# Routing of the expert stage: Silu times 1/x for the sigmoid, a power on GpSimd for 1/sqrt, PSUM operands and other places for VectorE's steps

## What is computed

```python
shared = silu(xf @ Ws_up) @ Ws_down
aff = xf @ centroids.T                       # xf: 4096 x 128, aff: 4096 x 64
_, idx = top_k(aff + expert_biases, 8)
w = sigmoid(take_along_axis(aff, idx, axis=1))
w = w / (sum(w, axis=-1, keepdims=True) + 1e-08)
cw = zeros((T, E)).at[arange(T)[:, None], idx].add(w)
h = silu(einsum('td,edf->etf', xf, W_up))    # 64 experts, F = 64
y = einsum('etf,efd->etd', h, W_down)
out = x + shared + einsum('etd,te->td', y, cw)
```

## Time and profile before

| | |
|---|---|
| median of 3 runs | 1102.46 us (1101.21 to 1103.21) |
| span of the profiled execution | 1102.4 us |
| its place among the runs | its own time is given by the span alone: 0.06 us below the median |
| TensorE busy | 948.5 us, 86% |
| VectorE busy | 845.6 us, 77% |
| ScalarE busy | 719.1 us, 65% |
| GpSimd busy | 446.7 us, 41% |
| expert stage | from 658.9 us to the end |

### The profile page before, as it was taken

How to read it: one execution, slowest core, us unless ns; L and a number is a source line. 1 busy time by engine, 2 the same in 40 slices (tenths; PEclk the granted TensorE clock), 3 DMA queues, 4 the chain that set the end, 5 groups by cost and what they waited for, 6 DMA issues and landing times.

```text
span 1102.4 us, 20447 instructions
## 1 busy us (share of the span) xinstructions
PE 948.5 (86%) x6019; PEld 747.6 (68%) x6052; DVE 845.6 (77%) x1938; ACT 719.1 (65%) x1416; POOL 446.7 (41%) x510
## 2 busy tenths in 40 slices
PE   4652099999658999999999979999999999999998
PEld 3541099999536677677767657676767676767676
DVE  6888177777567888888888657888787878787865
ACT  4650055555346877877777657777777778787776
POOL 1378650000156665565553403333333333333333
PEclk8655599999858999999999989999999999999999
DMA  8011122222210110100100008382838383838382
GB/s 250 26 49 61 50 57 67 63 65 66 66 32 21 30 30 23 33 25 24 35 21 20 1 7 194 71 207 62 189 80 196 73 189 74 192 77 192 79 193 72
DMA packets 63921, 89.99 MB, mean 82 GB/s; under 512 B 16559, under 2 KB 54610, under 8 KB 59730
## 3 DMA queue, kind: packets, MB, share of 16 engines
q1 hardware_dynamic: 59136, 80.33, 30.4%
q0 software_dynamic: 4096, 8.40, 2.7%
q10 hardware_dynamic: 594, 0.09, 0.0%
HBM read 70.90 MB, written 17.89 MB: 81 GB/s over the span
## 4 chain that ended last, share of the span: by engine, by line
PE 63%; DVE 12%; issue 7%; ACT 7%; POOL 7%; DMA 2%; SPq 1%; DVEq 0%; POOLq 0%; ACTq 0%
POOL xs L661 6%; PE ps L2146 4%; PE ps L2128 4%; PE ps L2130 4%; PE ps L2129 4%; PE ps L2148 4%; PE ps L2147 4%; PE ps L1932 3%; PE ps L1875 3%; PE ps L1956 3%; PE ps L1950 2%; PE ps L1995 2%; PE ps L1978 2%; PE ps L1854 2%; PE ps L1853 2%
## 5 line engine op out<-in xcount | busy, mean ns | idle before, releaser
L809 POOL TENSOR_TENSOR hl<-h,hh 128x512 fp32r<-128x512 f32 x128 | 165.6, 1294 | 292.1 <-ACT hh L1081 292.1
L1081 ACT ACTIVATE hh<-h 128x512 fp32r<-128x512 f32 (+1 forms) x264 | 165.1, 625 | 44.2 <-DVE h L1711 42.7
L1711 DVE TENSOR_TENSOR h<-ps,cwB 128x512 f32<-128x512 f32 x192 | 130.5, 680 | 45.3 <-ACT ps L1070 35.5
L1611 DVE TENSOR_REDUCE nm<-ps 128x4 f32<-128x512 f32 (+1 forms) x128 | 116.4, 951 | 35.7 <-PE ps L1978 33.8
L715 POOL DMA_INDIRECT yg<-ys,gps x64 | 63.0, 985 | 166.4 <-issue 155.9
L1070 ACT ACTIVATE ps<-ps 128x512 f32<-128x512 f32 x192 | 111.7, 582 | 26.2 <-PE ps L2130 25.6
L2146 PE MATMUL ps<-hh,wh 128*128 128x512 f32 x256 | 106.1, 414 | 11.4 <-DVE hl L1718 10.4
L2128 PE MATMUL ps<-xh,wh 128*128 128x512 f32 x256 | 105.0, 410 | 0.0
L2129 PE MATMUL ps<-xl,wh 128*128 128x512 f32 x256 | 101.6, 397 | 0.0
L2130 PE MATMUL ps<-xh,wl 128*128 128x512 f32 x256 | 101.4, 396 | 0.0
L2148 PE MATMUL ps<-hh,wl 128*128 128x512 f32 x256 | 101.3, 396 | 0.0
(11 more groups left out here) (326 smaller groups left out, 2692.3 us busy)
## 6 DMA issues: line engine op xcount, KB each, us to landing
cwB<-cwd SPq DMA_DIRECT2D x32, 1536.0 KB, 14.4
cwd<-cwS SPq DMA_DIRECT2D x64, 96.0 KB
xb<-xs SPq DMA_DIRECT2D x72, 64.0 KB, 1.8
ys<-yb SPq DMA_DIRECT2D x72, 64.0 KB, 1.6
x_res<-in_L_attn_x_dram SPq DMA_DIRECT2D x4, 512.0 KB, 6.8
wst<-in_L_ffn_W_up_dram SPq DMA_DIRECT2D x32, 64.0 KB, 2.2
wst<-in_L_ffn_W_down_dram SPq DMA_DIRECT2D x32, 64.0 KB, 1.9
out_dram<-y SPq DMA_DIRECT2D x8, 256.0 KB, 13.2
```

Source lines behind the costliest of these rows:

```text
L809: pool.tensor_tensor(hl4[:, slot(u), :], h4[:, slot(u), :], hh4[:, slot(u), :].bitcast(F32), op=ALU.subtract).then_inc(u_hlp, 1)
L1081: act.activation(hh4[r, slot(u), :], h4[r, slot(u), :], ACT.Copy).then_inc(u_hh, 1)
L1611: ins = dve.tensor_reduce(nm[:, u, 4 * g:4 * g + 4], o, axis=AX.X, op=ALU.max, negate=True)
L1711: dve.tensor_tensor(h4[:, slot(u), :], first, second, op=ALU.mult).then_inc(u_h, 1)
```

## The change

Tile 0's routing stays as it was. For the routings of tiles 1 to 7 (`first` is false):

- ScalarE takes Silu(x) of the logits instead of exp(-x), behind unit 17; VectorE divides by x (a reciprocal, L1564 before, and a multiplication more) to get the sigmoid. Logits so near to zero that adding 1e-20 gives 1e-20 are first moved off zero in two instructions (`near_zero`, `off_zero`). No table is loaded between the units.
- 1/sqrt(variance + 1e-5) is an addition and a power of -0.5 on GpSimd, behind its unit 5; ScalarE's ln and exp for it go.
- VectorE reads the tokens' low part, the logits and the biased logits directly from the PSUM bank; the copy of the logits goes. Since the low part now reads the bank that the logits overwrite, `x4_logits` on TensorE waits for it too (`d_hl`, named x4_parts).
- The last scaling writes the 48 columns that are spread straight to `cs` (`scaled`), and the rounding and the copy treat only the other 16 columns.
- The places move: normalization from behind unit 10 to 6, the transposes and their copy from 12 to 11, high and low part from 13 and 14 to 12 and 13, the reciprocal from 21 to 20, the last step from 28 to 27; logits stay at 14 and the transposes of the weights at 30.

```diff
@@ -22,6 +22,7 @@
 BIG = 1.0e30
+TINY = 1.0e-20
@@ -345,7 +347,7 @@
         SCATTERED = 16 * RT * K1
-        DVE_S, DVE_D = 4, 19
+        DVE_S, DVE_D, DVE_D1 = 4, 19, 20
@@ -437,6 +439,8 @@
             return bank[3] if isinstance(n, int) and n == 0 else bank[6]
+        X4_TURN, X4_LOGITS, X4_SILU, X4_SPREAD = 11, 14, 17, 30
@@ -802,12 +807,22 @@
+            def x4_rstd(n, p):
+                pool.wait_ge(d_mv, n + 1)
+                apart(pool, pool_passed)
+                pool.tensor_scalar(lnv[:, p, :], mv[:, p, :, 1], LN_EPS, None, ALU.add).then_inc(act_d, 1)
+                pool.wait_ge(act_d, n + 1)
+                pool.tensor_tensor(rstd[:, p, :], lnv[:, p, :], neg_half[:, :].broadcast_to([P, SUB]), op=ALU.pow).then_inc(d_rs, 1)
             def pool_tile(t, p, before, N, S):
                                        op=ALU.subtract).then_inc(u_hlp, 1)
+                    if u == 5 and S:
+                        x4_rstd(t + 2, p)
@@ -945,6 +960,10 @@
                 act.activation(g4[:, 0, :, :], af[:, :, :], ACT.Exp, scale=-1.0).then_inc(d_ex, 1)
+            def x4_silu(n):
+                act.wait_ge(d_afc, n + 1)
+                act.activation(g4[:, 0, :, :], af[:, :, :], ACT.Silu).then_inc(d_ex, 1)
@@ -1097,14 +1116,11 @@
                         out_copy4(before[0], before[1])
-                    if u == 12 and N:
+                    if u == X4_TURN and N:
                         x4_T(t + 1, 1 - p)
-                    if u == 16 and N:
-                        act.preload_act_table_set(TABLE)
-                        x4_exp(t + 1, 1 - p)
-                        if S:
-                            x4_rstd(t + 2, p)
-                    if u == 30 and N:
+                    if u == X4_SILU and N:
+                        x4_silu(t + 1)
+                    if u == X4_SPREAD and N:
                         x4_weights(t + 1, 1 - p)
@@ -1488,7 +1504,8 @@
-                own = Tickets(dve, dve_d, n * DVE_D)
+                first = isinstance(n, int) and n == 0
+                own = Tickets(dve, dve_d, 0 if first else DVE_D + (n - 1) * DVE_D1)
@@ -1504,8 +1521,52 @@
                     own.need(1)
-                    dve.tensor_tensor(xl4[:, p, :], flat(xnT4[:, :, :]), xh4[:, p, :].bitcast(F32),
+                    dve.tensor_tensor(xl4[:, p, :], flat(xnT4[:, :, :]) if first else x4_bank(n)[:, :], xh4[:, p, :].bitcast(F32),
                                       op=ALU.subtract).then_inc(d_hl, 1)
+                def logits():
+                    return x4_bank(n)[:, 0:SUB * E2].rearrange("p (k e) -> p k e", e=E2)
+                def near_zero():
+                    dve.wait_ge(d_af, n + 1)
+                    own.done(dve.tensor_scalar(g4[:, 2, :, :], logits(), TINY, TINY, ALU.add, ALU.is_equal))
+                def off_zero():
+                    own.need(own.n)
+                    dve.scalar_tensor_tensor(af[:, :, :], g4[:, 2, :, :], 2 * TINY, logits(), ALU.mult, ALU.add).then_inc(d_afc, 1)
+                def biased_logits():
+                    own.done(dve.tensor_tensor(bi[:, :, :], logits(), ebi[:, :].unsqueeze(1).broadcast_to([P, SUB, E2]), op=ALU.add))
+                def inverse_logits():
+                    dve.wait_ge(d_afc, n + 1)
+                    own.done(dve.reciprocal(g4[:, 3, :, :], af[:, :, :]))
+                def times_silu():
+                    dve.wait_ge(d_ex, n + 1)
+                    own.need(own.n)
+                    own.done(dve.tensor_tensor(g4[:, 4, :, :], g4[:, 2, :, :], g4[:, 0, :, :], op=ALU.mult))
+                def spread_columns():
+                    return cs[:, :, 0:EB].rearrange("p s (k h j) -> p s k h j", k=NPC, h=2)
+                def scaled():
+                    own.need(own.n)
+                    inverse = s4[:, 2, :].unsqueeze(2)
+                    own.done(dve.tensor_tensor(g4[:, 5, :, 0:EP], g4[:, 4, :, 0:EP], inverse.broadcast_to([P, SUB, EP]), op=ALU.mult))
+                    pairs = g4[:, 4, :, EP:E2].rearrange("p s (k j h) -> p s k h j", k=NPC, h=2)
+                    for half in range(2):
+                        dve.tensor_tensor(spread_columns()[:, :, :, half, :], pairs[:, :, :, half, :],
+                                          inverse.unsqueeze(3).broadcast_to([P, SUB, NPC, G]), op=ALU.mult)
+                def low_weights():
+                    own.need(own.n)
+                    dve.tensor_copy(cs[:, :, HB:HB + EP], cwh[:, :, 0:EP].bitcast(F32))
+                    dve.tensor_tensor(cs[:, :, HB + EP:HB + 2 * EP], g4[:, 5, :, 0:EP], cwh[:, :, 0:EP].bitcast(F32),
+                                      op=ALU.subtract).then_inc(d_cs, 1)
+                    assert own.n == DVE_D1, own.n
@@ -1560,12 +1621,18 @@
+                total = [then(lambda: dve.tensor_reduce(s4[:, 0, :], g4[:, 4, :, :], axis=AX.X, op=ALU.add)),
+                         then(lambda: dve.tensor_scalar(s4[:, 1, :], s4[:, 0, :], 1e-8, None, ALU.add)),
+                         then(lambda: dve.reciprocal(s4[:, 2, :], s4[:, 1, :]))]
+                if not first:
+                    return [norm, high, low, near_zero, off_zero, biased_logits, largest, replaced, chosen, inverse_logits,
+                            then(lambda: dve.tensor_tensor(g4[:, 2, :, :], g4[:, 3, :, :], g4[:, 1, :, :], op=ALU.mult)),
+                            times_silu, *total, scaled,
+                            then(lambda: dve.tensor_scalar(cwh[:, :, 0:EP], g4[:, 5, :, 0:EP], 0.0, None, ALU.add)), low_weights]
                 return [norm, high, low, affinity, biased, largest, replaced, chosen, sigmoid,
                         then(lambda: dve.tensor_tensor(g4[:, 4, :, :], g4[:, 3, :, :], g4[:, 1, :, :], op=ALU.mult)),
-                        then(lambda: dve.tensor_reduce(s4[:, 0, :], g4[:, 4, :, :], axis=AX.X, op=ALU.add)),
-                        then(lambda: dve.tensor_scalar(s4[:, 1, :], s4[:, 0, :], 1e-8, None, ALU.add)),
-                        then(lambda: dve.reciprocal(s4[:, 2, :], s4[:, 1, :])),
+                        *total,
                         then(lambda: dve.tensor_tensor(g4[:, 5, :, :], g4[:, 4, :, :],
@@ -1694,7 +1761,7 @@
-            STEP_AT = (10, 13, 14, 15, 16, 17, 18, 19, 20, 21, 22, 23, 24, 25, 26, 27, 28)
+            STEP_AT = (6, 12, 13, 15, 15, 16, 17, 18, 19, 20, 21, 22, 23, 24, 24, 25, 26, 27)
@@ -1910,6 +1978,8 @@
                 pe.wait_ge(d_Tc, n + 1)
+                if not (isinstance(n, int) and n == 0):
+                    pe.wait_ge(d_hl, n + 1)
                 for k in range(SUB):
@@ -2169,11 +2239,11 @@
                         out_T(before[0])
-                    if u == 12 and N:
+                    if u == X4_TURN and N:
                         x4_turned(t + 1, t if before is not None else None)
-                    if u == 14 and N:
+                    if u == X4_LOGITS and N:
                         x4_logits(t + 1)
-                    if u == 30 and N:
+                    if u == X4_SPREAD and N:
                         x4_weights(t + 1)
```

More of the change, by code:

```diff
@@ L90, in bass_two_layers @@
         eps_c = sb("eps_c", [P, 1], F32)
+        neg_half = sb("neg_half", [P, 1], F32)
         RT = 2 * SUB
@@ L622, in _ @@
             own.done(pool.memset(eps_c[:, :], LN_EPS))
+            own.done(pool.memset(neg_half[:, :], -0.5))
             own.done(pool.memset(zrow[:, :], 0.0))
@@ L1742, in dve_tile @@
             def dve_tile(t, p, before, N, S):
-                steps = dict(zip(STEP_AT, routing(t + 1, 1 - p))) if N else {}
+                steps = list(zip(STEP_AT, routing(t + 1, 1 - p))) if N else []
                 if before is not None:
@@ L1754, in dve_tile @@
                         result(*before)
-                    if u in steps:
-                        steps[u]()
+                    for at, step in steps:
+                        if at == u:
+                            step()
             tiles_of(dve, dve_tile)
```

## The result

| | before | with the change |
|---|---|---|
| median | 1102.84 us (1101.21 to 1103.21, 4 runs) | 1076.78 us (1076.07 to 1078.34, 4 runs) |
| profiled execution: time, span | not given, 1102.4 us | 1076.07 us, 1074.3 us |
| expert stage, from its first shared-expert matmul to the end | 443.5 us | 418.1 us |

The ratio is 0.9765, 95% interval 0.9751 to 0.9779: 26 us less. The forecast was 1087.3 with a range of 1079 to 1098. (With the change a span is 1.8 us shorter than the time of its execution. The forecast set the span of before equal to its median time; since the gain is a difference, nothing hangs on it.)

The account below looks back on a forecast made before the run. TensorE was taken as the bound, with idle time to give back. Per routing -3.85 + 1.0 + 0.8 = -2.05, seven times -14.3, and -0.8 once: -15.1 from 1102.4, so 1087.3 us, range 1079 to 1098.

Parts of the forecast that it names:

- A: TensorE's idle time at 748.02 in tile 1, behind ScalarE's 3.45 us break for table loads; goes, -1.56 us a routing.
- B: TensorE's idle time at 757.74 in tile 1, after VectorE's reciprocal; goes in its old form, -1.04 us a routing.
- The 1068: Time in us estimated from the skill page's 2.66 us a table switch, up to 2.7 us more gained per routing.
- C: TensorE's idle time at 765.56 in tile 1, waiting for the routing's last step; goes, -1.25 us a routing.
- The new wait at the logits: TensorE waits at the logits for VectorE's low part, 0.6 to 1.5 us; taken as +1.0 with its restart.
- The tail of the routing: VectorE's routing steps in units 16 to 27: 8.8 us of work against 8.1 spare; +0.8 a routing with restart.
- The three blocks: VectorE's product with Silu, addition of 1e-8 and rounding held up by GpSimd behind even units; 2.1 us together.
- The 1.2 for the scaling: In the tail, VectorE's scaling, now three operations, caught once more by GpSimd; 1.2 us at most.
- No wait in the tail: Rival: the scaling is not caught by GpSimd, only the logits' wait is left; 1080.3 us, chance 0.20.
- sign of being wrong: A GpSimd row of rstd over 1 us and waits of TensorE at units 6, 7 or 11.
- the rule: GpSimd's idle time covers about 1 us for `xm`, 2 for `hl`; beyond it each us costs TensorE one.
- `xm`: Tile 0's only wait for `xm` goes because the step stands four units earlier; -0.8 us once.

Follow-up runs that it names:

- e5: Changed kernel with VectorE's operands, widths and places as before, except the reciprocal behind unit 20, and the off-zero instructions kept; ratio 0.9837.
- e4: Changed kernel with 1/sqrt again as ln and exp on ScalarE behind unit 17, with two table loads, in six of the seven routings; ratio 0.9957.
- e3: Changed kernel with TensorE's logits behind unit 15 instead of 14; ratio 0.9683, expert stage 409.3 us.
- e10: Kernel of e3 with the weights wh and wl alone moved down by 32 bytes; ratio 0.9748, expert stage 413.7 us.
- e2: Changed kernel with the constant -0.5 in eps_c's 32 bytes, so every other tensor keeps its address from before; ratio 0.9795, expert stage 423.1 us.
- e6: Changed kernel with two more powers of the same size on GpSimd ahead of the one that counts, in six tiles; ratio 0.9811, expert stage 419.6 us.

## Why the prediction was wrong

*A, the table loads.* Right in kind. The break is gone, and with it A. As a term it was too small: e5 shows that without ScalarE's break B does not come either. I had both, A and B, in the sum, so the total did not suffer. The drain of some 1380 ns that the Trainium skill (ScalarE: Activation LUTs, What ACT_TABLE_LOAD costs) adds to each load is in no row: in e4 a load starts at 748.77 and the next activation at 750.06, 1.29 later, as long as the load's own record. The 1068 that was estimated from it did not occur either.

*B.* It went, but "the reciprocal at 753.87 takes 1.74, and B follows" named as the cause what e5 shows to be harmless without the break before it.

*C.* Went with the shorter and earlier steps; e5, which has neither, keeps it. Its price was too small, as e5 and e3 show.

*The new wait at the logits.* 1.0 forecast; 6.2 us in seven waits are 0.89, with the 0.17 of each 1.06. The high part (L1520, 0.42) was not blocked, so VectorE did come first, and GpSimd's subtraction beside it grew to 1.49 and ran until 730.37. VectorE's `hl`, started at 730.11, took 0.80 instead of 0.68. Right by the waits, but they are not the whole cost. e10 has the pace of before and no wait at the logits: its stage is 413.7, 9.4 us below e2's, so the wait cost 1.35 a routing.

*The tail of the routing.* **This step failed.** I added 0.8 a routing for work that would come through, 5.6 us in all; TensorE waits for nothing there. The three blocks cost 0.56, 0.55 and 0.50 (0.98, 0.72 and 0.70 less the 0.42, 0.17 and 0.20 of free ones; the last is an estimate between 0.17 for 4 and 0.28 for 256 columns of such an operation), 1.6 instead of 2.1. The 1.2 for the scaling was put in at its upper bound, and it did not occur: VectorE was first, and GpSimd waited. 5.5 + 1.6 = 7.1 stays under the 8.1 that VectorE may use by the same working. The rival "No wait in the tail" had it.

*GpSimd.* The power takes 1.04, not 0.6. That was named as a sign of being wrong, together with waits of TensorE at units 6, 7 or 11, and no such wait came: it costs nothing that the waits show, as forecast. The price put on a slower one was too high: e6 has 1.5 us where the rule gave 6 to 12.

*The sum.* -15.1 less the 5.6 of the tail is -20.7. e2, which is the change without the shift, has -20.4 in the stage. That this is so close is in part luck. A, B, C and `xm` were priced at 27.8 in all, and e10 has 29.8; the logits were priced at 7.0, and e2 against e10 has 9.4. The two errors cancel.

*What no step had.* **This failed too.** The shift of the tokens and hidden parts by 32 bytes is worth 5.0 us of the 25.4, and the sum had 0. I had written that "no part of the change removes one of these matmuls" and taken their pace as given; the line that adds a 4-byte constant was costed at nothing by not being looked at. Without it the time would have been some 1082 (1080 by e2's ratio), in the range; with it the range is missed by 2 us. I had no row of before that shows another pace, and the granted clock of tile 1 was 1.00 in both, so a price could not have been worked out from the profile. The place of the operands could have been seen to change, though.

## What to carry to other kernels

When one engine's break makes the others late, waits behind it may be its consequence, as B was and C was not: take the break away first, and do not give a later wait a cause of its own merely because a long instruction stands next to it. Where a sum sets work against spare time, do not put every possible block in at its upper bound as the likely value. And a new small tensor moves every one behind it: compare the busy time of one unchanged stretch (here the last tile) before attributing a difference to the logic of a change.

## What was not expected of the hardware

- Weights and streamed operand of TensorE that begin alike modulo 64 bytes in SBUF: 0.227 us a matmul of 512 columns; 32 bytes apart: 0.233. The granted clock was 1.00 in both, 2.4 GHz. Weights at 0 and operand at 0 is as fast as 32 and 32. Modulo 128 would fit the same runs.
- GpSimd's power on 128 x 4 numbers takes 1.04 us, 0.81 more than its addition of the same size (0.23).
- The block between GpSimd and VectorE goes both ways: at 751.41 GpSimd's subtraction took 1.39 instead of 1.29, while VectorE's scaling ran from 751.09 to 751.64, and at 728.88 it took 1.49 beside VectorE's high part, which had started 0.08 before.
